# A Mamba, attention and expert kernel on one core: other first steps, a divided last product, new tables of half-steps

## What is computed

```python
def mamba_block(x, ...):                     # first layer, followed by attention_block
    xz = rmsnorm(x, norm_m_w) @ in_proj_w.T  # 512 columns
    x_ssm, z = jnp.split(xz, 2, axis=-1)     # 256 and 256
    x_ssm = silu(causal depthwise conv, 4 taps, of x_ssm, + conv_b)
    ssm_p = x_ssm @ x_proj_w.T               # 16 columns B, 16 columns C, 1 dt
    delta = softplus(dt_raw @ dt_w.T + dt_b)
    A = -exp(A_log)                          # 256 x 16
    h = exp(delta * A) * h + delta * B * x   # over time, for 256 channels x 16 states
    y = sum over states of h * C + x * D_skip
    return x + (y * silu(z)) @ out_proj_w.T
def attention_block(x, ...):                 # 4 heads of 32, 2 of keys and values, causal
    x = x + softmax(q @ k.T * scale + causal) @ v @ o_w.T
    return x + (silu(xn @ gate_w.T) * (xn @ up_w.T)) @ down_w.T
def L0_ffn(x): return layernorm(gelu(x @ ternary(W_fc))) @ ternary(W_proj)
def L1_attn(x): ...                          # a second Mamba block of the same sizes
def L1_ffn(x): ...                           # 8 experts; each token goes to one of them
```

## Time and profile before

| | |
|---|---|
| Three runs | 784.50, 785.26, 788.36 us; median 785.26 |
| Profiled execution | 786.48 us, its span 784.6 us |
| Instructions | 9754 |
| Mean granted clock of PE | 0.89 |
| First product of the loop starts | 29.44 us |
| Last scan ends | 676.75 us |
| Memory read and written | 88.91 MB and 3.11 MB |

### The profile page before, as it was taken

The page is one execution under the profiler, slowest core; times in us unless marked ns, Lnnn a source line. Parts: engine busy times, 40 slices in busy tenths (PEclk is TensorE's granted clock), DMA queues, the critical chain, the costliest instruction groups (busy, mean ns, idle before and its releaser), DMA issues. The chain is left out here.

```text
span 784.6 us, 9754 instructions
## 1 busy us (share of the span) xinstructions
PE 609.4 (78%) x3318; PEld 402.9 (51%) x3318; DVE 593.3 (76%) x613; ACT 479.5 (61%) x869; POOL 420.3 (54%) x233
## 2 busy tenths in 40 slices
PE   7477685868779879898789977897577486778996
PEld 3043453546435455444545545444444365568996
DVE  1588999789958968778797976987888699553442
ACT  3658852866496786777967887677936544012331
POOL 0166954454552665634666346755865666405773
PEclk9689876988988979999999997999899879878998
...
GB/s 125 294 226 14 333 99 1 3 319 125 13 15 141 280 25 1 1 0 273 174 1 0 31 378 39 0 1 273 160 0 4 359 71 109 3 138 168 238 237 52
DMA packets 35948, 92.67 MB, mean 118 GB/s; under 512 B 7523, under 2 KB 13146, under 8 KB 35898
## 3 DMA queue, kind: packets, MB, share of 16 engines
...
HBM read 88.91 MB, written 3.11 MB: 117 GB/s over the span
## 5 line engine op out<-in xcount | busy, mean ns | idle before, releaser
L491 POOL TENSOR_TENSOR hc<-hst,bc 128x1024 f32<-128x1024 f32 x128 | 301.5, 2360 | 257.7 <-DVE hst L994 130.5
L629 ACT ACTIVATE dA<-delta,m_A_s 128x511 f32<-128x511 f32 x256 | 173.9, 712 | 41.7 <-DVE hst L1001 33.3
L1329 PE MATMUL bank<-ident,hc 128*128 128x128 f32 x1024 | 150.4, 296 | 41.2 <-POOL hc L491 41.2
L1329 PEld LDWEIGHTS bank<-ident,hc 128*128 128x128 f32 x1024 | 128.9, 154 | 77.5 <-POOL hc L491 59.4
L1001 DVE TENSOR_TENSOR_SCAN hst<-dA,bank 128x1024 f32<-128x1024 f32 x68 | 155.3, 2284 | 3.3 <-issue 1.7
L977 DVE TENSOR_TENSOR bank<-bank,bc 128x1024 f32<-128x1024 f32 x68 | 83.7, 1231 | 17.0 <-DMA bc<-crows 7.4
L994 DVE TENSOR_TENSOR_SCAN hst<-dA,bank 128x512 f32<-128x512 f32 x60 | 73.2, 1220 | 2.1
L988 DVE TENSOR_TENSOR_SCAN hst<-dA,bank 128x512 f32<-128x512 f32 x60 | 72.8, 1214 | 0.9
L1242 PE MATMUL bank<-arena 128*32 128x128 f32 (+4 forms) x480 | 57.5, 366 | 12.7 <-ACT arena L719 7.5
L1242 PEld LDWEIGHTS bank<-arena 128*32 128x32 f32 (+2 forms) x480 | 31.6, 153 | 38.4 <-issue 17.0
L1242 PE MATMUL bank<-ht,bc 128*128 128x128 f32 x368 | 46.3, 281 | 0.7 <-ACT ht L881 0.7
...
## 6 DMA issues: line engine op xcount, KB each, us to landing
bc<-crows SPq DMA_DIRECT2D x128, 512.0 KB, 8.9
bc<-in_w SPq DMA_DIRECT2D x23, 512.0 KB, 3.6
...
conv<-in_m_cw SPq DMA_DIRECT2D x2, 512.0 KB, 3.6
...
arena<-rows_out,source POOLq DMA_INDIRECT x23, 3.7
out_rows<-zs,target POOLq DMA_INDIRECT x23, 2.7
```

Source lines behind the costliest of these rows:

```text
L491: pool.tensor_tensor(hc[:, g % HCRING], hst[:, g % HRING], bc[:, p, 1], ALU.mult) \
L629: act.activation(dA[:, g % RING, j, 1:], delta[:, h, 1:], ACT.Exp, scale=M[mamba_of(c)]["A"][:, h, n:n + 1]).then_inc(sems["dA"], 1)
L1329: last = pe.matmul(bank[:, YB, P * j:P * j + P], hc[:, g % HCRING, n, P * j:P * j + P], ident[:], start=False, stop=s % PAIRS == PAIRS - 1 ...
```

## The change

Three pieces of code and the tables.

1. *Start, half 0.* PE makes only the projection of half 0, by one matmul with winx0; ACT copies it with the last tap as its scale; DVE adds the three other taps, one after the other, into the same tile; ACT puts silu on the sum. Half 1 is as before. The fold of half 0 for the later blocks is made by DVE at half-step 3 (conv of 4 x 128 columns, multiplied with winx0).
2. *Start, first pair.* PE spreads the rows of pair 0, two of B and two of C, with a column of the identity as weight; DVE copies the B rows, ACT the C rows into `bc`. SP leaves pair 0 of block 0 out.
3. *End.* Of the last pair POOL multiplies state 0 and DVE state 1. The last projection is in two matmuls of their own: half 0 stands ahead of the transposes of half 1, and the sum is in bank DU.
4. *Tables.* Every one is made anew, most numbers by one or two. Among them: in TAIL and FAT, GELU of sequence 0 one later (FAT[0] gelu 23 to 24), the gates of half 1 later by one in most blocks; in A_START[1] score tiles 1 and 2 from 10 and 14 to 14 and 17; the silus of block 3 (HEAD[3] visit) from 18 to 21; FAT[3] x2 from 33 to 35; in HEAD[7] xp from 27 to 25 and visit from 27 to 28; NSTART (the norms of sequences 1 to 3) one or two later; HEAD[1] raw1 from 12 to 11.

```diff
-TAIL = (dict(ycp1=3, back1=4, gate1=4, out=6, res=7, ycp0=19, back0=32, gate0=33), dict(ycp1=3, back1=4, gate1=4,
...
+TAIL = (dict(ycp1=2, back1=4, gate1=5, out=5, res=6, ycp0=19, back0=31, gate0=32), dict(ycp1=3, back1=4, gate1=5,
...
-NSTART = {1: 1, 2: 13, 3: 25}
-LATE_AT = 24
-Z_FIRST = (33, 38)
...
+NSTART = {1: 3, 2: 14, 3: 27}
+LATE_AT = 25
+Z_FIRST = (34, 35)
...
+        def rows_in(c, p):
+            return 32 * BC_OF.count(BC_OF[p]) * (c + 1) - (32 if p == 0 else 0)
...
+        folds = [(conv[:], d[f"m{m}_cw"].unsqueeze(0).to_broadcast([P, TAPS, HALVES * P])) for m in range(2)]
+        early = [folds[0], (norm_m[:], d["norm_m"]), (taps[:], d["m0_taps"])] + weights_of(0)[0]
...
+        W_SCALED, FOLDED_1, A0_MADE, TAPPED, SPREAD, FOLDED_0, A1_MADE = 4, 5, 6, 9, 11, 12, 13
...
-                for p in range(PAIRS):
+                for p in range(0 if c else 1, PAIRS):
...
-                            pool.wait_ge(sems[BC_OF[p]], 32 * BC_OF.count(BC_OF[p]) * (g // STEPS + 1))
+                            if g == 0:
+                                pool.wait_ge(sems["setup_act"], 4)
+                            else:
+                                pool.wait_ge(sems[BC_OF[p]], rows_in(g // STEPS, p))
                         if g >= HCRING:
                             pool.wait_ge(sems["yacc"], g - HCRING + 1)
-                        pool.tensor_tensor(hc[:, g % HCRING], hst[:, g % HRING], bc[:, p, 1], ALU.mult) \
-                            .then_inc(sems["hc"], 1)
+                        states = slice(0, 1 if g == LAST - 1 else 2)
+                        pool.tensor_tensor(hc[:, g % HCRING, states], hst[:, g % HRING, states], bc[:, p, 1, states],
+                                           ALU.mult).then_inc(sems["hc"], 1)
...
-                act.activation(xs_of(0, h), bank[:, (HB, FB5)[h], :], ACT.Silu, bias=M[0]["cb"][:, h:h + 1]) \
-                    .then_inc(sems["park"], 1)
+                if h == 0:
+                    act.activation(xs_of(0, 0), bank[:, HB, :], ACT.Identity, bias=M[0]["cb"][:, 0:1],
+                                   scale=taps[:, TAPS - 1:TAPS]).then_inc(sems["setup_act"], 1)
+                    act.wait_ge(sems["setup_dve"], TAPPED)
+                    act.activation(xs_of(0, 0), xs_of(0, 0), ACT.Silu).then_inc(sems["park"], 1)
+                else:
+                    act.activation(xs_of(0, 1), bank[:, FB5, :], ACT.Silu, bias=M[0]["cb"][:, 1:2]) \
+                        .then_inc(sems["park"], 1)
             act.preload_act_table_set(EXP_LN)
             project_rows(0)
             softplus(0, 0)
-            act.wait_ge(sems["setup_dve"], 5)
+            act.wait_ge(sems["setup_dve"], A0_MADE)
             for g in range(AHEAD):
                 for j in range(2):
                     decay(g, j)
+                    if g == 0:
+                        act.wait_ge(sems["setup_pe"], 3 + j)
+                        act.activation(bc[:, 0, 1, j], bank[:, (YB, FB5)[j], :], ACT.Copy).then_inc(sems["setup_act"], 1)
...
-                if h == 0:
-                    dve.wait_ge(sems[BC_OF[p]], 32 * BC_OF.count(BC_OF[p]) * (c + 1))
+                if g == 0:
+                    dve.wait_ge(sems["setup_dve"], SPREAD)
+                elif h == 0:
+                    dve.wait_ge(sems[BC_OF[p]], rows_in(c, p))
...
+                    out_bank = DU if c == BLOCKS - 1 else HB
                     dve.wait_ge(sems["out"], c + 1)
                     if c < SEQS:
                         dve.wait_ge(sems["n_xl"], c + 1)
-                    dve.tensor_tensor(x3[:, k], bank[:, HB, :], x3[:, k], ALU.add).then_inc(sems["res"], 1)
+                    dve.tensor_tensor(x3[:, k], bank[:, out_bank, :], x3[:, k], ALU.add).then_inc(sems["res"], 1)
...
+                    if b == 0 and t == 3:
+                        dve.wait_ge(sems["setup_dve"], W_SCALED)
+                        dve.tensor_tensor(conv[:, :, 0:P], conv[:, :, 0:P],
+                                          winx0[:, 0:P].unsqueeze(1).to_broadcast([P, TAPS, P]), ALU.mult) \
+                            .then_inc(sems["setup_dve"], 1)
...
-            dve.scalar_tensor_tensor(conv[:], conv[:], norm_m[:],
-                                     winx0.unsqueeze(1).to_broadcast([P, TAPS, HALVES * P]), ALU.mult, ALU.mult) \
+            dve.tensor_scalar(winx0[:, 0:P], winx0[:, 0:P], norm_m[:], None, ALU.mult).then_inc(sems["setup_dve"], 1)
+            dve.scalar_tensor_tensor(conv[:, :, P:], conv[:, :, P:], norm_m[:],
+                                     winx0[:, P:].unsqueeze(1).to_broadcast([P, TAPS, P]), ALU.mult, ALU.mult) \
                 .then_inc(sems["setup_dve"], 1)
             dve.wait_ge(sems["n_rs2"], 1)
             dve.tensor_tensor(xn0[:, 0], bank[:, SB6, :], nst, ALU.mult).then_inc(sems["n_xn"], 1)
             minus_A(0)
+            for back in range(1, TAPS):
+                if back == 1:
+                    dve.wait_ge(sems["setup_act"], 2)
+                else:
+                    dve.wait_ge(sems["setup_dve"], TAPPED - TAPS + back)
+                x = xs_of(0, 0)
+                dve.scalar_tensor_tensor(x[:, back:], bank[:, HB, 0:T - back], taps[:, TAPS - 1 - back:TAPS - back],
+                                         x[:, back:], ALU.mult, ALU.add).then_inc(sems["setup_dve"], 1)
+            for j in range(2):
+                dve.wait_ge(sems["setup_pe"], 1 + j)
+                dve.tensor_copy(bc[:, 0, 0, j], bank[:, (YB, FB5)[j], :]).then_inc(sems["setup_dve"], 1)
...
+                    if g == LAST - 1:
+                        dve.wait_ge(sems["scan"], LAST)
+                        dve.wait_ge(sems["yacc"], LAST - HCRING)
+                        dve.tensor_tensor(hc[:, g % HCRING, 1], hst[:, g % HRING, 1], bc[:, PAIRS - 1, 1, 1], ALU.mult) \
+                            .then_inc(sems["half"], 1)
...
+                if c == 0 and h == 0:
+                    mm(bank[:, HB, :], winx0[:, 0:P], xn_of(0)).then_inc(sems["raw"], 1)
+                    return
+                if c == 1 and h == 0:
+                    pe.wait_ge(sems["setup_dve"], FOLDED_0)
...
+                    pe.wait_ge(sems["setup_act"], 4)
...
+                    if g == LAST - 1 and n == 1:
+                        pe.wait_ge(sems["half"], 2 * len(SINGLE) + 1)
...
+            def project_first_half():
+                pe.wait_ge(sems["gate"], 2 * BLOCKS - 1)
+                pe.wait_ge(sems["dbu"], LAST)
+                mm(bank[:, DU, :], M[1]["wo"][:, 0, :], zs[:, (BLOCKS - 1) % 2, 0], True, False)
+
+            def project_second_half():
+                pe.wait_ge(sems["gate"], 2 * BLOCKS)
+                mm(bank[:, DU, :], M[1]["wo"][:, 1, :], zs[:, (BLOCKS - 1) % 2, 1], False, True).then_inc(sems["out"], 1)
+
             def project_out(c):
                 pe.wait_ge(sems["gate"], 2 * c + 2)
                 for h in range(HALVES):
@@ -1350,9 +1410,14 @@
 
             def tail(c, h, t):
                 if t == TAIL[c][f"back{h}"]:
+                    if h == 1 and c == BLOCKS - 1:
+                        project_first_half()
                     turn_back(c, h)
                 if h == 1 and t == TAIL[c]["out"]:
-                    project_out(c)
+                    if c == BLOCKS - 1:
+                        project_second_half()
+                    else:
+                        project_out(c)
...
-            pe.wait_ge(sems["setup_dve"], 4)
+            pe.wait_ge(sems["setup_dve"], W_SCALED)
             raw(0, 0)
+            pe.wait_ge(sems["setup_dve"], FOLDED_1)
             raw(0, 1)
             warm(3)
             x_project(0)
             warm(4)
             dt_half(0, 0)
-            warm(5)
+            pe.wait_ge(sems["second_loaded"], 16 * len(second))
+            pe.wait_ge(sems["park"], 2)
+            for kind in range(2):
+                for j in range(2):
+                    if kind == 1:
+                        pe.wait_ge(sems["setup_dve"], SPREAD - 1 + j)
+                    row = STATE * kind + j
+                    mm(bank[:, (YB, FB5)[j], :], ident[0:BCR, row:row + 1].to_broadcast([BCR, P]), prow[0:BCR, :]) \
+                        .then_inc(sems["setup_pe"], 1)
```

82 lines of the change are left out of this document (41 added, 41 removed).

## The result

| | before | after |
|---|---|---|
| Runs | 784.88 us median (783.84 to 788.36, 4 runs) | 759.13 us median (756.98 to 761.04, 4 runs) |
| Ratio | | 0.9662, 95% interval 0.9643 to 0.9680 |
| Profiled execution, span | 784.6 | 757.8 |
| First scan | 31.18 | 28.95 |
| Fifth product | 47.34 | 44.42 |

The kernel is 26 us faster; 12 were forecast, with a range that ended at 761. The three stretches of the sum gave 5.2 us up to the ninth product (forecast 4.2), 21.0 in the middle (forecast 7) and 0.8 at the end (forecast 0.7).

The account below looks back on a forecast made before the run. DVE's chain of products and scans was taken as the bound, idle for 97.9 us in the middle. Gains of 2.4 + 1.8 + 0.7 + 7 = 11.9 us gave a median of 773.4, range 761 to 784.

Parts of the forecast that it names:

- First convolution half: Start: half 0 by one matmul; ACT's second silu ends at 16.7 instead of 19.20, all behind it 2.5 us earlier.
- First scan: Start: PE spreads the first pair's rows, then ACT's roots hold the first scan, at 29.3 instead of 31.18.
- Fold: DVE's second pair: folding the second half's taps costs 0.7 us free, 1.8 when it waits for POOL; 1.8 taken.
- rival of a free port: Start and end: the fold and the half product run beside POOL, giving 771.9 us; chance 0.15.
- Fifth product: Start: it could start at 44.9 instead of 47.34, no wait for rows left; 2.4 us gained.
- Ninth product: Its 2.38 us wait for ACT's copy of du: 1.8 counted as gained, bounds 0 and 2.4.
- End: Last pair split between POOL and DVE, projection in two matmuls: 0.7 us gained, 0.4 to 1.1.
- Tables: Middle of the loop, new half-step numbers: 7 us gained of 12 counted, bounds -4 and 22.
- The four named waits: DVE's waits at 285.20, 236.58, 571.66 and 383.71: gains of 3, 4.5, 3 and 1.5 us, sum 12.
- The upper bound: Tables' gain in the middle: at most 22 us, all four named waits (22.3) gone.
- tables give it all: Rival for the middle: the four named waits vanish, giving 758.1 us; chance 0.14.
- PE parked: Rival, slower: PE stands at block 7's row projection before ACT's silus and the scan waits; 798.4 us, chance 0.08.

Follow-up runs that it names:

- a_nospread: Kernel after with rows of the first pair through memory again, without the copies on DVE and ACT; ratio to the kernel before 0.9661, last scan ends 653.26 us.
- b_newtab: Kernel before with all tables of half-steps as after and nothing else; ratio to the kernel before 0.9722, last scan ends 654.27 us.
- p_qk: Kernel before with queries and keys of sequence 0 projected one half-step earlier; gains 4.4 us between pairs 20 and 24, keeps 3.0 at pair 40.

## Why the prediction was wrong, point by point

- **First convolution half: right.** Second silu done by 16.7; it ended at 16.51. Delta was done at 22.95, not 23.6: the second copy of rows ended at 22.34, ahead of the 22.9 to 24.8 allowed (PE spread the two B rows in 1.91 us, as at full clock).
- **First scan: right, with two errors that cancel in part.** 29.3 forecast, 28.95 measured, held by the root. Delta was 0.65 us earlier, and the root 5.36 behind it instead of 5.0. a_nospread confirms that the copies delay the root (1.5 us).
- **Fold: right by the row taken.** 1.8 us for 1.74. The trace agrees with the rule cited (the Trainium skill, SBUF — State Buffer, Who interferes with whom) for a step with two inputs in SBUF: 0.66 or 1.74 us by which engine was first, and at the end POOL's half held up by DVE's. The rival of a free port falls. The gate at 651.18, with one input in PSUM, took its 0.68 beside POOL.
- **Fifth product: right** (44.9; 44.42, no wait for rows).
- **Ninth product: nearly right, with its place misread.** 4.2 us forecast, 5.2 measured, all 2.38 of the wait gone. But these are no gain of the new code alone: with the old tables 0.5 is left, and the new tables without it give 0.6 (63.61). The sum counted 2.4 + 1.8 as the code's and should have asked what holds the ninth product when DVE comes earlier: ACT's copy, whose time the table of block 1 sets.
- **End: right.** 0.7 forecast, 0.8 measured, with one half waiting for the other and the second, halved projection.
- **Tables: the step that failed.** 7 us forecast, 21.0 measured; the tables alone are worth 22.5 (b_newtab). The four named waits gave about what was taken for them (7.1 by place, 10.2 at the last scan), though two by more than counted and two by little or nothing: that 7 and 7.1 agree is partly luck. The error is what was done with the other 38 waits: they were put at no gain, and new waits were set against the four, by counting steps whose producer stands in a later half-step (23 before, 33 after). By that count the idle time should have grown elsewhere; it fell by 22 us in all. That such a step costs only where the producing engine is late fits this, but no run tests it. One place of gain, PE's 6.02 us at 129.99, stood in the trace; it is no wait of DVE's, so it wasn't among the 42, but it made the 4.03 us at 141.85 that were (p_qk has no wait there). Looking only at DVE's waits and not at what stood behind PE's own was worth 3 to 4 us here.
- **The upper bound was too small.** 22 us was the sum of the four waits. The changed tables touched all 42, so the bound was their sum, 85.8 us. The prediction put all 97.9 us of idle time into the 42 waits; 12 of them are the short gaps, which stay. The rival "tables give it all" (758.1) lies nearest to the result (759.13), but not by its reason: at the places of three of the four waits DVE still stands 3.63 and 3.92, 2.84 and 1.37 us. What is left open is which neighbours carry the other 10 us of the tables.
- **PE parked: it happened and held up no scan.** After the change PE waits 3.79 us for the silus of block 7 (576.97), POOL 4.89 for PE; no scan of DVE's waits for POOL there. Delta of that block waits 4.39 instead of 3.28.
